# A top-1 expert feed-forward stage: rows in four loads, two down products moved, one power for two blocks in four pairs, three roots on ScalarE

## What is computed

```python
# x: (8, 128, 128), flattened to x_flat (1024, 128)
router_probs = softmax(x_flat @ gate_w)              # 8 experts
expert_idx = argmax(router_probs); expert_w = router_probs[expert_idx]
for e in range(8):
    h = gelu(x_flat @ w1[e] + b1[e])                 # exact gelu, 128 -> 512
    y = h @ w2[e] + b2[e]                            # 512 -> 128
    out = out + where(expert_idx == e, expert_w, 0)[:, None] * y
x = layernorm(x_flat + out)                          # (x - mean) / sqrt(var + 1e-5)
```

## Time and profile before

| | |
|---|---|
| median of 3 runs | 201.82 us (200.45 to 203.16) |
| the profiled execution | 203.06 us, of which the span that the trace covers is 201.3 us |
| sort of the rows (first to last indirect DMA issued) | 152.4 to 164.0 us of the span |
| loads of the rows issued from | 166.7 us |
| last store issued at | 198.00 us |
| granted TensorE clock, 160 to 195 us | 1.00 |

### The profile page before, as it was taken

One profiled execution on the slowest core, in us unless ns is written; L12 is line 12 of the kernel. 1 busy time (PEld: TensorE's weight loads), 2 busy tenths in 40 slices (PEclk: granted clock), 3 DMA queues, 4 the chain that ended last, 5 costly groups with the idle time before them and its releaser, 6 DMA issues. The chain is left out here.

```text
span 201.3 us, 11917 instructions
## 1 busy us (share of the span) xinstructions
PE 175.7 (87%) x5244; PEld 153.5 (76%) x5244; DVE 123.8 (61%) x363; ACT 97.0 (48%) x264; POOL 68.7 (34%) x129
## 2 busy tenths in 40 slices
PE   0998996999999999739999999999899969899940
PEld 0986884767666769639899888999799759899940
DVE  0232798499998280235899893242579803988881
ACT  2422882569787446412343343322245617566750
POOL 6180000557565300000000001810226740689884
PEclk9999999999999999985999999999999999999996
DMA  5944000000000000000000000005960858787300
GB/s 178 373 125 141 7 0 0 0 10 3 0 3 0 3 3 7 3 3 3 0 0 0 2 2 0 7 3 165 352 101 26 250 144 224 200 215 234 97 8 4
DMA packets 15632, 14.57 MB, mean 72 GB/s; under 512 B 1350, under 2 KB 12001, under 8 KB 15603
## 3 DMA queue, kind: packets, MB, share of 16 engines
q1 hardware_dynamic: 14867, 13.10, 23.1%
q0 software_dynamic: 736, 1.06, 1.5%
HBM read 12.08 MB, written 2.53 MB: 73 GB/s over the span
## 5 line engine op out<-in xcount | busy, mean ns | idle before, releaser
L564 PE MATMUL banks<-V 32*32 32x64 f32 x1664 | 37.6, 231 | 6.0 <-issue 4.3
L564 PEld LDWEIGHTS banks<-V 32*32 32x32 f32 x1664 | 33.7, 107 | 8.6 <-issue 7.9
L570 PE MATMUL banks<-MM,WT 32*32 32x64 f32 x1536 | 35.8, 233 | 0.0
L570 PEld LDWEIGHTS banks<-MM,WT 32*32 32x32 f32 x1536 | 30.8, 107 | 0.0
L1154 DVE SCALAR_TENSOR_TENSOR MM<-V,banks 128x512 f32<-128x512 f32 x24 | 16.5, 686 | 18.1 <-PE banks L564 17.6
L949 ACT ACTIVATE V<-banks 128x512 f32<-128x512 f32 x20 | 11.9, 597 | 24.4 <-PE banks L570 24.4
L387 POOL MEMSET WT<- 128x1950 f32 x1 | 1.7, 1723 | 57.5 <-PE banks L570 57.5
L1019 ACT ACTIVATE GG<-banks,b1T 128x128 f32<-128x128 f32 x60 | 16.9, 378 | 5.6 <-PE banks L848 5.6
L848 PE MATMUL banks<-qkl,GG 128*128 128x128 f32 x120 | 15.9, 277 | 2.5 <-DVE qkl L1400 1.8
L848 PEld LDWEIGHTS banks<-qkl,GG 128*128 128x128 f32 x120 | 14.5, 192 | 3.1 <-DVE qkl L1400 2.0
L827 PE MATMUL banks<-E,GG 128*128 x120 | 16.3, 279 | 0.5 <-ACT GG L1019 0.5
(11 more groups left out here) (217 smaller groups left out, 401.0 us busy)
## 6 DMA issues: line engine op xcount, KB each, us to landing
GG<-in_L_ffn_w SPq DMA_DIRECT2D x15, 256.0 KB
wqkv<-in_L_attn_w_qkv SPq DMA_DIRECT2D x3, 512.0 KB, 5.3
Tt<-padded_taps SPq DMA_DIRECT2D x1, 1024.0 KB, 5.7
sorted_tokens<-WT SPq DMA_DIRECT2D x1, 975.0 KB, 13.5
GG<-in_L_ffn_b SPq DMA_DIRECT2D x15, 64.0 KB
WT<-sorted_tokens SPq DMA_DIRECT2D x1, 585.0 KB, 4.6
x_sb<-in_x SPq DMA_DIRECT2D x1, 512.0 KB, 4.0
wfc<-in_L_attn_w_fc SPq DMA_DIRECT2D x1, 512.0 KB, 6.9
```

What stands on the lines that cost most here:

```text
L564: return mm(bank[PV_BANKS[k % RING]][quad(q), 64 * n:64 * n + 64], V[quad(q), g, 0, :], V[quad(q), g], start=True, stop=True)
L570: return mm(bank[QM_BANKS[k % RING]][quad((q + 2) % 4), 64 * n:64 * n + 64], Q[quad(q), g, :], MM[quad(q), g], start=True, stop=True)
```

## The change

Rows: four loads, blocks 4 and 5, then 0 to 3, then 6 and 7, then 8 to 14. SP reads the expert numbers of blocks 4 to 7 at once, ahead of the first weights of 4 and 5, issues three of the loads of rows, then the first weights of 6, biases of 4 and 5, first weights of 7, the fourth load of rows, biases of 6 and 7. From block 8 on all is as it was.

TensorE: `down(2)` and `down(3)` both stand ahead of the wait for the rows of block 4. Turn 4 is then transpose, up. Turn 5 is transpose, up. From turn 6 on the order is as before.

Powers: blocks 2 and 3, 4 and 5, 6 and 7, 8 and 9 share one power instruction each, which waits for the variance of the second of them. VectorE norms such a pair together, after the variance of the block behind the pair. Block 12 has its root on ScalarE, with the blocks 13 and 14.

```diff
-LOADS = ((NS, 6), (0, NS), (6, NB))
-POWERS = NB - 2
+LOADS = ((NS, 6), (0, NS), (6, 8), (8, NB))
+POWERS = NB - 3
+PAIRED = (2, 10)
...
             sp.wait_ge(expert_ready, 2)
-            experts += expert_numbers(mybir.EngineType.SP, EARLY, EARLY + 2)
+            experts += expert_numbers(mybir.EngineType.SP, EARLY, W1_SLOTS)
             for j in range(EARLY, EARLY + 2):
                 first_weights(j)
+
+            def rows(n):
+                lo, hi = LOADS[n]
+                sp.dma_start(xs[:, lo:hi, :], slot_rows(xs_dram)[:, lo:hi, :]).then_inc(xs_loaded[n], 16)
+
             sp.wait_ge(xs_sent, 16 * B)
-            for n, (lo, hi) in enumerate(LOADS):
-                sp.dma_start(xs[:, lo:hi, :], slot_rows(xs_dram)[:, lo:hi, :]).then_inc(xs_loaded[n], 16)
-            for j in range(EARLY, EARLY + 2):
-                second_bias(j)
-            for j in range(EARLY + 2, NB):
+            for n in range(3):
+                rows(n)
+            first_weights(6)
+            second_bias(4)
+            second_bias(5)
+            first_weights(7)
+            rows(3)
+            second_bias(6)
+            second_bias(7)
+            for j in range(W1_SLOTS, NB):
                 experts += expert_numbers(mybir.EngineType.SP, j, j + 1)
                 first_weights(j)
                 second_bias(j)
...
-            def slot_deviation(j):
-
-                pool.wait_ge(slot_var, j + 1)
-                nc.gpsimd.tensor_tensor(stat("rstd", j, 1), stat("sd", j, 1), stat("mhalf"), ALU.pow
-                                        ).then_inc(slot_rstd, 1)
-
-            slot_deviation(0)
+            def slot_deviation(lo, hi):
+                pool.wait_ge(slot_var, hi)
+                nc.gpsimd.tensor_tensor(stat("rstd", lo, hi - lo), stat("sd", lo, hi - lo),
+                                        stat("mhalf").broadcast_to([P, hi - lo]), ALU.pow).then_inc(slot_rstd, hi - lo)
+
+            slot_deviation(0, 1)
             for j in range(NB):
-                if j + 1 < POWERS:
-                    slot_deviation(j + 1)
-                pool.wait_ge(number_ready, B + (2 if j < 6 else 3))
+                if PAIRED[0] <= j + 1 < PAIRED[1]:
+                    if j % 2 == 1:
+                        slot_deviation(j + 1, j + 3)
+                elif j + 1 < POWERS:
+                    slot_deviation(j + 1, j + 2)
+                pool.wait_ge(number_ready, B + (2 if j < 6 else 3 if j < 8 else 4))
...
             for s in range(NB + 2):
+                if s == NS:
+                    down(NS - 2)
+                    down(NS - 1)
                 if NS <= s < NB:
                     tokens_transposed(s)
+                if NS + 2 <= s < NB:
                     down(s - 2)
...
-                if j == 6:
-                    rows_loaded(2)
+                if j in (6, 8):
+                    rows_loaded(2 if j == 6 else 3)
...
-                if j >= 1:
+                if PAIRED[0] < j <= PAIRED[1]:
+                    if j % 2 == 0:
+                        normed(j - 2)
+                        normed(j - 1)
+                elif j >= 1:
                     normed(j - 1)
```

## The result

| | before | after |
|---|---|---|
| median of 20 runs each | 202.76 us | 204.76 us |
| ratio after / before | | 1.0108 (95% interval 1.0076 to 1.0141) |
| the profiled execution, its span | 203.06, 201.3 | 205.12, 203.1 |
| from VectorE's number conversion of rows 0 to 3 to the last store | 198.00 - 170.20 = 27.80 | 199.82 - 170.41 = 29.41 |

The ratio compares only the fast executions, those within 1.5% of the fastest of their kernel; one execution of 249 us before and one of 417 us after are among those left out.

A forecast was written before the change was run, and what follows sets the result against it. GpSimd was taken to bound the kernel after the sort. Power at 176.85 plus 21.12 gave a last store at 197.97 against 198.00, so execution stays about 203.1, less 1.24: 201.8 us, range 200.5 to 203.2.

The forecast's parts named there:

- GpSimd closes behind it: From the sort to the end: TensorE (1.90 us a turn) began ahead, so GpSimd (1.83 a turn) ends last.
- VectorE's turn is shorter than both: Expert blocks: VectorE needs less time per turn than GpSimd's 1.83 us and TensorE's 1.90.
- GpSimd's own work: Power of block 2 to last store: 23.00 less 2.45 for five powers, plus 0.57 for wide ones, gives 21.12 us.
- the straight line: Two-column power on GpSimd: second column costs 0.14 us, 0.43 / 3 between one and four columns; duration near 0.72.
- The start: Behind the sort: late bias of block 4 moves the power of 2 and 3 to 176.85 from 175.00.
- SP and the rows: SP's loads: moved biases and rows cost nothing; two more expert numbers are covered by 1.36 us of idle time.
- The tail: Blocks 12 to 14: block 12 normed at 194.85 behind the table load, last store at 198.0.
- the rival of the waiting store: End of the kernel: GpSimd waits for the last store, whose start costs 0.79; slower by 0.7 (202.5 us), chance 0.12.
- the drain rival: ScalarE's table load: 1.38 us of drain delays block 12's norm; slower by 1.35 (203.2 us), chance 0.03.
- The dear power: GpSimd's wide power costs as much as four columns, 1.72 instead of 0.57; slower by 1.15 (203.0 us), chance 0.09.
- the late rows: SP's longer reading pushes the loads 2 us back, VectorE 1.0 late (202.8 us), chance 0.03.
- the first: ScalarE's and VectorE's idle time until about 165 does not come back; faster by about 1.0 (200.8 us), chance 0.25.

The follow-up runs named there:

- third root alone: The kernel before with only block 12's root moved to ScalarE: 27.82 us from the rows, ratio 1.0014 (0.9964 to 1.0064).
- pairs alone: The kernel before with only the shared powers and norms by two for blocks 2 to 9: 28.90 us from the rows, ratio 0.9991 (0.9936 to 1.0046).
- pairs as single powers: The kernel before with both powers of a pair as one-column instructions ahead of its two neighbouring stores, norms in pairs: 29.83 us from the rows, 203.17 us.
- the old order: The changed kernel with TensorE's order as it was before, all else kept: 28.58 us from the rows, ratio 0.9987 (0.994 to 1.0034).

## Why the prediction was wrong

**What bounds.** "GpSimd closes behind it" was right for before. "VectorE's turn is shorter than both" was right too, and it hid the weak place. After a late release VectorE has to catch up, and it does so slowly. Without waits it goes from the bias of 10 to that of 11 in 190.05 - 188.21 = 1.84 with two norms between, and in about 1.4 where no norm is between, 1.6 on average against TensorE's 1.90. So a delay of 1.0 takes three to four blocks to make good, and the next comes before or just when it is: block 4 by the order, 6 and 10 by the stores, then the power of block 10. VectorE becomes the engine that sets the end.

**GpSimd's own work, the step that failed.** "So a power costs GpSimd 0.49 net", and five powers fewer give 2.45. As GpSimd's time that is right, and the wide power measured 0.72, as taken from the straight line (0.72 to 0.76 in the other pairs). But the same 0.49 is the difference between a gap of 0.8 and one of 0.3 between stores, and I read it as pure cost. In the profile after, the stretch from the shared power to the last store is 199.82 - 177.02 = 22.80, not 21.12. Those 1.68 are the error of the sum (the start was 0.17 later than said). GpSimd's own idle time holds them: stores 4, 8 and 12 waited 0.93, 1.21 and 0.57 for their norms where 0.3 lies between neighbours, 1.81 more together. What made those norms late are the waits that the sum lacks on VectorE, 1.07 and 0.99, and the 0.91 ahead of norm 10 that follows from the second, together with the norms by two, which stand behind the variance of one more block. No run tells these two shares apart.

**A second term too small: the start of a store that waits.** The norm of block 4 ended at 182.10 + 0.34 = 182.44 and its store started at 183.29, 0.85 later; store 8 started 0.85 behind its norm, store 12 0.86. In every profile here a store that GpSimd stood waiting for started 0.85 to 0.92 behind its norm. The prediction took 0.10, from the store at 157.77. GpSimd was not held there: its DMA before ended at 157.46, so this one started after the usual 0.31.

The wait ahead of norm 10 deserves a reading of its own. Norms by two come after the variance of the block behind the pair. Store 8 waits 1.21 for norm 8, the power of block 10 stands behind store 8 in GpSimd's program, and VectorE waits 0.91 for that power. It is a circle through two engines. I had asked what each wait delays, but not what is queued behind the store that waits.

**The start.** Predicted: bias of 4 late by about 1.0, power of 2 and 3 at 176.85. Measured: a wait of 0.89, the power at 177.02. With the rows 0.2 later, this is right. That this lateness is a cost of its own, 0.37 with no pairs, I had not said: I set it only against the pairs' gain.

**SP and the rows.** Priced at nothing, measured at nothing (27.75 against 27.80 with the loads alone).

**The tail.** Block 12's norm was to start at 194.85 and started at 196.03. That is VectorE's lateness and not the table's, since the root was done at 194.86. The norm ended at 196.37 and GpSimd, which was waiting for it, started the store at 197.23, 0.86 later. I had taken 0.10 and left 0.79 to the rival of the waiting store, which was nearer. Two more stores behind it bring 199.82. Of the last store's 1.82 over the forecast, 1.18 is the late norm and 0.76 the dear start, less 0.1 that the instructions from this norm to that of block 14 were shorter (2.59 instead of 2.70). In before GpSimd was still behind at that point and did not pay it in the tail. The third root alone costs nothing (+0.02). ScalarE in after:

```profile
193.37 1.28 ACT L1045 ACT_TABLE_LOAD   x1
194.66 0.20 ACT L1048 ACTIVATE st<-st 128x1 f32<-128x1 f32 x1
```

The root starts 0.01 behind the load. The Trainium skill, "ScalarE: Activation LUTs", section "What ACT_TABLE_LOAD costs", would have another 1.38 here. Neither this trace nor that of the kernel with the third root alone agrees with it, so the drain rival falls.

**The rivals.** The dear power (it took 0.72), the drain and the late rows did not occur. The waiting store came true three times, for stores 4, 8 and 12, but only because VectorE was late; its forecast, once at the end, gave 202.5. The rival that held the right rows was the first. It saw ScalarE and VectorE idle until 165.1 on a release that the trace could not name, and asked only whether this could go away. The question to put to it was what GpSimd did at that time, and where the change would make it do the same again. It issued indirect DMAs 0.3 us apart, and the pairs do just that. None of my cases was a loss by this, so the range ended at 203.2, too low.

No version tried beats before: the shortest stretch is 27.75, against 27.77 and 27.80 for before.

## What to carry to other kernels

Taking an instruction of 0.5 us off a saturated engine can be worth nothing or less if it was what stood between two indirect DMAs; price what its gap did for the other engines, and what a start behind a wait costs instead of a start in a row, and ask of each engine how fast it makes a delay good. An idle time that the trace can't explain is a row to build on: look at what all other engines do while it lasts, and whether the change repeats that. When an operation is shared by two blocks, follow the second block's wait through every queue behind it, back to the engine that started it.

## What the runs showed of the hardware

- While GpSimd issues indirect DMAs 0.3 us apart, TensorE's releases to VectorE and ScalarE arrive late: 1.43 and 0.87 in after, 3.2 behind the last six of the sort, 0.03 for block 10 where the second store is left out. They mostly come 0.4 to 0.7 after the end of the second store; one came ahead of it (pairs alone: transpose started at 183.12, copy at 184.25, second store 183.50 to 184.48). With a power between the stores (0.8 apart) no release was over 0.3 late. With a multiplication of 0.21 (0.4 apart) it was (0.80).
- In after, its repeat, pairs alone, pairs as single powers and the old order, every product or transpose that ended between the start of a second neighbouring store and 0.2 behind its end, and for which an engine stood waiting, was released late. One transpose that ended in the gap ahead of it was too (the one of 183.12), others there came at most 0.11 late. What ended during the first was not seen to be hit: in before the product of block 14 ended at 194.27, during the first of the last neighbours (194.04), and its bias began at 194.31.
- TensorE itself runs on meanwhile. TensorE's ends are modelled in the profile, so a lateness of a few hundredths says nothing. By which path the release is held stays open: no run separated the issuing of the DMA from the traffic that it starts.
- An indirect store that GpSimd stood waiting for started 0.85 to 0.92 behind the end of the norm that released it; in a row of such DMAs the next starts 0.3 behind the end of the one before.
- A power on GpSimd takes 0.58 for one column, 0.72 to 0.76 for two and 1.01 to 1.10 for four. The lower figures make 0.14 per column on top of 0.44.
